# Windowed attention of a fused transformer kernel: from four windows of 32 queries against 64 keys to two halves of 64 queries against 96 keys

## The reference

```python
for i in range(6):
    x = attn_layer(shift_tokens(x), Wqkv[i], q_scale[i], k_scale[i], Wo[i]) + x
    x = ffn_layer(shift_tokens(x), ln_g[i], ln_b[i], W1[i], b1[i], W2[i], b2[i]) + x

def local_attention(q, k, v):            # w = 32, nw = n // 32
    bk2, bv2 = (look(bk), look(bv))      # each window of 32 keys behind the window before it
    ...
    mask = (it < jb) | (it > jb + w) | (jb == -1)
    sim = jnp.einsum('bhwie,bhwje->bhwij', bq, bk2) * QK_SCALE
    attn = jax.nn.softmax(jnp.where(mask, -max, sim), -1)
    return jnp.einsum('bhwij,bhwje->bhwie', attn, bv2)
```

## Time and the profile before

| | us |
|---|---|
| median of 3 runs | 3318.39 |
| lowest and highest | 3317.79, 3320.12 |
| the profiled execution, its own time | 3320.12 |
| its span, from the first to the last instruction | 3318.0 |
| mean granted clock of PE | 0.911 of full speed |
| steady state, four visits of the last stage | 67.68 |
| the last stage, about | from 1634 to 3315 |

### The profile page before, as it was taken

One profiled execution on the slowest core, in us unless ns is written; L12 is line 12 of the kernel. 1 busy time (PEld: TensorE's weight loads), 2 busy tenths in 40 slices (PEclk: granted clock), 3 DMA queues, 4 the chain that ended last, 5 costly groups with the idle time before them and its releaser, 6 DMA issues.

```text
span 3318.0 us, 85682 instructions
## 1 busy us (share of the span) xinstructions
PE 2877.0 (87%) x35131; PEld 1723.7 (52%) x35188; DVE 2383.9 (72%) x4250; ACT 1882.8 (57%) x5278; POOL 1208.9 (36%) x851
## 2 busy tenths in 40 slices
PE   4669857475979799999689999999999999999997
PEld 3444546452334423333256666666666666666664
DVE  4950279627960487777588888888888888888885
ACT  4222231126422246666468777787778777787775
POOL 0010000100000011111157766766776676676662
PEclk7569855587989989999889999999999999999999
DMA  2000000000000110000222233222332332322222
GB/s 101 2 1 0 36 2 3 1 1 0 0 0 0 34 44 25 24 22 22 92 63 66 65 76 93 62 72 64 97 77 65 97 77 66 95 61 62 60 65 51
DMA packets 48229, 153.18 MB, mean 46 GB/s; under 512 B 11552, under 2 KB 13856, under 8 KB 45952
## 3 DMA queue, kind: packets, MB, share of 16 engines
q1 hardware_dynamic: 47872, 148.11, 17.0%
HBM read 43.53 MB, written 5.44 MB: 15 GB/s over the span
## 4 chain that ended last, share of the span: by engine, by line
PE 65%; DVE 26%; ACT 2%; DVEq 2%; issue 2%; DMA 1%; POOLq 1%; ACTq 1%; SPq 0%; POOL 0%
PE ps L1481 10%; PE ps L648 7%; PE ps L1532 6%; PE ps L1499 5%; PE ps L1540 5%; DVE arena L1942 4%; DVE arena L972 4%; PE ps L1076 4%; PE ps L1104 4%; PE ps L1553 4%; PE ps L1091 3%; PE ps L1514 2%; PE ps L1559 2%; DVE arena L2022 2%; DVE pack_l L1935 2%
## 5 line engine op out<-in xcount | busy, mean ns | idle before, releaser
L1481 PE MATMUL ps<-arena 128*128 128x512 f32 x1152 | 560.2, 609 | 17.5 <-ACTq L1761 16.2
L2099 POOL TENSOR_TENSOR arena<-arena 128x1024 f32<-128x1024 f32 x190 | 448.3, 2360 | 145.5 <-DVE arena L1911 143.5
L1826 ACT ACTIVATE arena<-ps,arena 128x64 f32<-128x64 f32 x1536 | 457.0, 324 | 47.2 <-DVE arena L2022 44.1
L2105 POOL TENSOR_TENSOR arena<-arena 128x2048 f32<-128x2048 f32 x95 | 344.3, 3624 | 224.9 <-ACT arena L1768 219.8
L1241 DVE TENSOR_REDUCE arena<-ps 128x1 f32<-128x512 f32 x512 | 329.3, 685 | 77.2 <-PE ps L1076 72.1
L1203 ACT ACTIVATE arena<-ps 128x1024 f32<-128x1024 f32 x256 | 262.2, 1024 | 178.5 <-PE ps L1091 169.8
L1826 ACT ACTIVATION_READ_ACCUMULATOR arena<-ps,arena 128x1 f32 x1536 | 333.5, 217 | 0.0
L1906 DVE TENSOR_TENSOR arena<-ps,arena 128x1024 f32<-128x1024 f32 x192 | 235.0, 1224 | 110.1 <-PE ps L1481 95.6
L1481 PEld LDWEIGHTS ps<-arena 128*128 128x128 f32 x1152 | 197.0, 191 | 172.5 <-issue 158.0
L191 POOL TENSOR_SCALAR rstd<-mv 128x4 f32<-128x4 f32 x32 | 8.2, 255 | 718.4 <-DVE mv L178 718.4
L1532 PEld LDWEIGHTS ps<-arena 128*64 128x64 f32 x6144 | 189.6, 138 | 111.3 <-issue 111.3
(11 more groups left out here) (286 smaller groups left out, 5490.1 us busy)
## 6 DMA issues: line engine op xcount, KB each, us to landing
arena<-pack_l SPq DMA_DIRECT2D x144, 256.0 KB
arena<-grow SPq DMA_DIRECT2D x144, 256.0 KB
arena<-in_deep SPq DMA_DIRECT2D x6, 2649.5 KB, 10.7
arena<-pack_l SPq DMA_DIRECT2D x96, 128.0 KB
arena<-grow SPq DMA_DIRECT2D x84, 128.0 KB
arena<-in_rotary SPq DMA_DIRECT2D x6, 1024.0 KB, 7.5
pack_tern<-in_tern SPq DMA_DIRECT2D x2, 2888.0 KB, 10.7
arena<-scr_q SPq DMA_DIRECT2D x96, 48.0 KB
```

The source lines that it names most:

```text
L1481: last = T.matmul(m.ps[0:rows.stop - rows.start, at + half, :], f.xs[t % 2][:, rows], w.wqkv[:, j * INNER + half * BLK:j * INNER + (half + ...
L1826: last = A(f.prob[:, p, :], m.ps[:, 4 + j % 2, i * SPAN:(i + 1) * SPAN], ACT.Exp, bias=f.nmax[t % 2][:, p:p + 1], accum_out=f.rsum[t % 2][ ...
L2099: G.tensor_tensor(f.rot[t % 2][:, here], f.rot[t % 2][:, here], f.sin[:, here], ALU.add)
L2105: G.tensor_tensor(r, r, spread(f.ss[t % 2], DH), ALU.mult).then_inc(s["rotated"], 1)
```

## The change

The queries are taken in two halves of 64 instead of four windows of 32. A half sees 96 keys: its own 64 and the 32 before them, and the mask removes what lies outside the band. The scores of a bank hold 4 x 96 columns in place of 4 x 64. A head's probabilities are now one matrix of 128x96, which needs a transpose of its own, and comes out with keys on partitions 0 to 95, just as `heads` wants them: no spreading, one copy of 96x1024 for eight heads. The eight transposes of a `probs` call fill banks 0 and 1 together, and so PE waits before `probs(1)` until ACT has copied what `probs(0)` left there. Values need 96 rows a half, with two or three DMAs a visit. The heads' order inside the probabilities is that of the banks.

```diff
-    "const": [("ident", P), ("band", 64), ("band0", 64), ("cT", 2 * LAYERS)],
+    "const": [("ident", P), ("band", 96), ("band0", 96), ("cT", 2 * LAYERS)],
...
-SPAN = 2 * WIN
+SPAN = WIN + HALF
+ORDER = [h for half in range(2) for odd in range(2) for h in range(8 * half + odd, 8 * half + 8, 2)]
...
-    return sum(4 + (u % BT != 0) for u in range(t % 2, t + 1, 2))
+    return sum(2 + (u % BT != 0) for u in range(t % 2, t + 1, 2))
...
         for i in range(GROUP):
-            for w in range(WINS):
+            for half in range(2):
                 for e in range(2):
-                    k = 2 * j + i
-                    rows, queries = slice(DH * e, DH * e + DH), slice(WIN * w, WIN * (w + 1))
-                    last = T.matmul(m.ps[queries, 4 + e, i * SPAN:(i + 1) * SPAN], f.qT[rows, k, queries],
-                                    f.kT[t % 2][rows, k, WIN * w:WIN * w + SPAN], start=False, stop=True,
+                    h = ORDER[GROUP * (j + e) + i]
+                    rows = slice(DH * e, DH * e + DH)
+                    last = T.matmul(m.ps[HALF * half:HALF * (half + 1), 4 + e, i * SPAN:(i + 1) * SPAN],
+                                    f.qT[rows, h // 2, HALF * half:HALF * (half + 1)],
+                                    f.kT[t % 2][rows, h // 2, HALF * half:HALF * half + SPAN], start=False, stop=True,
                                     skip_group_check=True)
...
     def probs(j):
-
-        for i in range(GROUP):
-            last = T.transpose(m.ps[:, PROB_AT + j, i * P:(i + 1) * P], f.flat_prob[:, 4 * j + i, :], m.ident)
+        for i in range(8):
+            last = T.transpose(m.ps[0:SPAN, PROB_AT + i // 4, (i % 4) * P:(i % 4 + 1) * P], f.prob[:, 8 * j + i, :],
+                               m.ident)
...
-                                    f.v[t % 2][:, half, h * DH:(h + 1) * DH],
-                                    f.pT[:, h, HALF * half:HALF * (half + 1)], start=True, stop=True)
+                                    f.v[t % 2][0:SPAN, half, h * DH:(h + 1) * DH],
+                                    f.pT[0:SPAN, ORDER.index(h), HALF * half:HALF * (half + 1)], start=True, stop=True)
...
         if behind:
+            pe.wait_ge(s["p_copied"], 2 * t - 1)
             pe.wait_ge(s["normed"], 2 * t)
             probs(1)
...
-        for e in range(2):
-            for u in range(2):
-                to, got = f.turned_probs(0, e, u)
-                last = A(to, got, ACT.Copy)
-        last.then_inc(s["p_copied"], 1)
+        A(f.pT[0:SPAN, 0:8, :], wide(PROB_AT, SPAN).rearrange("p a (i b) -> p (a i) b", b=P),
+          ACT.Copy).then_inc(s["p_copied"], 1)
...
-    for u in range(2):
-        V.memset(f.pT_windows[SPAN * u:SPAN * (u + 1), :, :, 1 - u, :], 0.0)
...
-        for e in range(2):
-            for u in range(2):
-                to, got = f.turned_probs(1, e, u)
-                last = V.tensor_copy(to, got)
-        last.then_inc(s["p_copied"], 1)
+        V.tensor_copy(f.pT[0:SPAN, 8:16, :],
+                      m.ps[0:SPAN, PROB_AT:PROB_AT + 2, :].rearrange("p a (i b) -> p (a i) b", b=P))\
+            .then_inc(s["p_copied"], 1)
...
-        sp.dma_start(v[t % 2][WIN:SPAN, 0, :], raw[0:WIN, :]).then_inc(s["v_spread"][t % 2], 16)
-        sp.dma_start(v[t % 2][SPAN:P, 0, :], raw[0:SPAN, :]).then_inc(s["v_spread"][t % 2], 16)
-        sp.dma_start(v[t % 2][0:SPAN, 1, :], raw[WIN:WIN + SPAN, :]).then_inc(s["v_spread"][t % 2], 16)
-        sp.dma_start(v[t % 2][SPAN:P, 1, :], raw[HALF:P, :]).then_inc(s["v_spread"][t % 2], 16)
+        sp.dma_start(v[t % 2][WIN:SPAN, 0, :], raw[0:HALF, :]).then_inc(s["v_spread"][t % 2], 16)
+        sp.dma_start(v[t % 2][0:SPAN, 1, :], raw[WIN:P, :]).then_inc(s["v_spread"][t % 2], 16)
```

More of the change, by code:

```diff
@@ L1439 @@
 WIN = 32
-WINS = P // WIN
 HALF = P // 2
-SPAN = 2 * WIN
+SPAN = WIN + HALF
 KEYS = WIN + P
 FRONT = WIN + 1
+ORDER = [h for half in range(2) for odd in range(2) for h in range(8 * half + odd, 8 * half + 8, 2)]
 GROUP = 4
@@ L1509, in scores @@
         for i in range(GROUP):
-            for w in range(WINS):
+            for half in range(2):
                 for e in range(2):
-                    k = 2 * j + i
-                    rows, queries = slice(DH * e, DH * e + DH), slice(WIN * w, WIN * (w + 1))
-                    last = T.matmul(m.ps[queries, 4 + e, i * SPAN:(i + 1) * SPAN], f.qT[rows, k, queries],
-                                    f.kT[t % 2][rows, k, WIN * w:WIN * w + SPAN], start=False, stop=True,
+                    h = ORDER[GROUP * (j + e) + i]
[3 more added lines that the diff above has]
+                                    f.kT[t % 2][rows, h // 2, HALF * half:HALF * half + SPAN], start=False, stop=True,
                                     skip_group_check=True)
-                    if i == GROUP - 1 and w == WINS - 1:
+                    if i == GROUP - 1 and half == 1:
                         last.then_inc(s["scored"], 1)
     def probs(j):
-        for i in range(GROUP):
-            last = T.transpose(m.ps[:, PROB_AT + j, i * P:(i + 1) * P], f.flat_prob[:, 4 * j + i, :], m.ident)
+        for i in range(8):
+            last = T.transpose(m.ps[0:SPAN, PROB_AT + i // 4, (i % 4) * P:(i % 4 + 1) * P], f.prob[:, 8 * j + i, :],
+                               m.ident)
         last.then_inc(s["p_made"], 1)
@@ L1824, in exponentials @@
             for i in range(GROUP):
-                p = 8 * (j // 2) + 2 * i + j % 2
+                p = GROUP * j + i
                 last = A(f.prob[:, p, :], m.ps[:, 4 + j % 2, i * SPAN:(i + 1) * SPAN], ACT.Exp,
@@ L2021, in maxima @@
             dve.wait_ge(s["scored"], 4 * t + j + 1)
-            V.tensor_reduce(f.nmax[t % 2][:, 8 * (j // 2):8 * (j // 2) + 8].rearrange("p (i e) -> p e i", e=2)[:, j % 2, :],
+            V.tensor_reduce(f.nmax[t % 2][:, GROUP * j:GROUP * (j + 1)],
                             m.ps[:, 4 + j % 2, 0:GROUP * SPAN].rearrange("p (h k) -> p h k", h=GROUP), AX, ALU.max,
@@ L2237, in deep_setup @@
     f.pT = a.take(LH * P).rearrange("p (a b) -> p a b", b=P)
[L2238 to L2248, removed]
+    f.prob = a.take(LH * SPAN).rearrange("p (a b) -> p a b", b=SPAN)
     f.kT = [a.take(QB * KEYS).rearrange("p (a b) -> p a b", b=KEYS) for _ in range(2)]
@@ L2481, in band_masks @@
 def band_masks():
-    i, j = np.arange(P)[:, None], np.arange(2 * WIN)[None, :] - WIN
-    seen = (j <= i % WIN) & (j >= i % WIN - WIN)
-    first = seen & ((j >= 0) | (i >= WIN))
+    i, j = np.arange(P)[:, None], np.arange(96)[None, :] - 32
+    seen = (j <= i % 64) & (j >= i % 64 - 32)
+    first = seen & ((j >= 0) | (i >= 64))
     big = np.float32(-1e30)
```

## The result

The changed kernel takes 3380.4 us (median of four runs, 3378.4 to 3385.4) where the kernel before takes 3318.4 us (median of four as well): 1.019 times as long, with a 95% interval of 1.0175 to 1.020. The forecast was 3375 us.

A forecast was written before the change was run, and what follows sets the result against it. TensorE's own work list plus one 0.40 us wait per visit bounds the kernel. Stretch A +0.05 and stretch B +0.55 make +0.60 us a visit, +57 us over 95 visits: 3375 us, range 3342 to 3425 us.

The forecast's parts named there:

- Transposes: Sixteen probability transposes a visit in place of eight: +0.44 us in stretch A and +0.44 us in stretch B.
- Bands: Four bf16 band matmuls a visit grow from 256 to 384 columns: +0.11 us in each stretch.
- Scores: Score products, half as many and wider: 0.79 us a call as before, so 0, between -0.14 and +0.64 us.
- Rivals 1 and 2: Score calls at the heads' rate, 1.01 us (3417 us, chance 0.15); row halves not overlapping, 1.43 us (3497 us, chance 0.06).
- rival 3: Score calls cost by the instruction, 0.39 us a call: -8 us, 3311 us; chance 0.06.
- lower end of 3346 us: Low end of the forecast's own span: 0.65 us a score call, stretch A -0.12 us, stretch B +0.41 us.
- Heads: Head products contract 96 rows in place of 128, with the same moving columns: 0, between -0.1 and 0.
- The DVE path: VectorE's work through stretch A: copies -0.50 us, two maxima +0.27 us, from 3.87 to 3.64 us.
- Stretch A: Part of a visit from first band matmul to first head product, 3.87 us: +0.05 us, between 0 and +0.10.
- Stretch B: Rest of the visit, where TensorE never waits: bands +0.11, scores 0, transposes +0.44, together +0.55 us.
- The new wait: TensorE waits before the second transposes for ScalarE's copy of the first: 0.7 us of cover, cost 0.
- Work beside PE: ScalarE about 0 net, GpSimd +1.05 us and VectorE +0.27 us in free time, DMAs and memsets 0.

The follow-up runs named there:

- experiment 3: Changed kernel with every second probability transpose left out (output isn't the reference's): 3308.1 us, 0.9975 of the kernel before.
- experiment 4: Kernel before with each probability transpose issued twice to the same place: 3421.0 us, 1.031.
- 10: Changed kernel with each of its sixteen probability transposes a visit issued twice to the same place: 3546.0 us, 1.0688 of the kernel before.
- experiment 1: Changed kernel with the old score products, 32 of 32 queries against 64 keys per call on eight tiles: 3386.5 us, 1.0206 of the kernel before.
- experiment 2: Changed kernel with the second group of transposes in PSUM banks of its own, without the wait for ScalarE's copy: 3379.8 us, 1.0188 of the kernel before.
- experiment 5: Kernel before with two bf16 matmuls of 512 columns ahead of each group of four probability transposes: 3420.7 us, 1.0308.
- 7: Kernel before with the four copies of the second probabilities shared, two on VectorE and two on ScalarE: 3296.3 us, 0.993.
- 8: Kernel before with the copies shared between VectorE and ScalarE, and VectorE's two ahead of its second maxima: 3292.1 us, 0.9924.
- experiment 6: Kernel before with VectorE copying the second probabilities before its second maximum: 3315.3 us, 0.9994.

## Why the prediction was right, by its steps

- **Transposes** (+0.44 us in A, +0.44 in B): measured +0.42 to 0.44 and +0.44, +78 us over the stage. Experiments 3, 4 and 10 move the time by this term alone, down and up. This is the cause of the slowdown; the other terms together are -16 us.
- **Bands** (+0.11 and +0.11): +0.11 and +0.11, 20 us.
- **Scores** (0, between -0.14 and +0.64): +0.03 a call, 5 us. The nearest row was L1104's, four tiles. Rivals 1 and 2 would have shown 1.01 and 1.43 us, rival 3 0.39 us; the row is 0.82. Experiment 1 ran both shapes in the same surroundings, 0.79 and 0.82 us. There was some luck in 0.79 as a forecast: its rule, the stream and 0.14 us on top, would give 0.43 + 0.14 = 0.57 us for the old shape, which takes 0.79. So the rule held for four tiles and not for eight, and what sets a call's time is not shown. The prediction's lower end of 3346 us also has a slip: by its own sum A would be -0.09 and not -0.12 us, hence 3349 us.
- **Heads** (0): 2.02 us from start to start before and after, 191.7 us over the stage in both.
- **The DVE path** (3.87 to 3.64 us): 3.66 us in the median visit, measured where it binds, in experiment 3. Maxima grew by 0.135 us each (predicted 0.135), the copy takes 1.22 us as predicted.
- **Stretch A** (+0.05, between 0 and 0.10): +0.10, the upper end. I took the middle between two readings of PE's idle time (0.45 and 0.55 us); the scores' 0.03 and that choice make up the difference. This and the scores in B are the 5 us between 3375 and 3380.
- **Stretch B** (+0.55): 2.68/4 - 0.10 = +0.57.
- **The new wait** (0.7 us of cover, cost 0): cost 0, as experiment 2 shows, but with 1.66 us of cover (0.7 predicted). The step was wrong in one sign. I let ACT's copy start 0.44 us later because the transposes end later. ACT isn't waiting for them, it is busy until 2413.25 with two copies of 1.02 us of the turned keys and queries (L1778, L1780), and those follow `turn_rotated`, which comes before the added transposes; so relative to the bands the copy starts 0.44 us earlier. It changed nothing only because both answers are above zero.
- **Work beside PE** (0): the groups by line of ACT, DVE and PE's transposes (busy us, mean ns, idle before):

```profile
L1828 ACT ACTIVATE arena<-ps,arena 128x96 f32<-128x96 f32 x1536 | 497.9, 350 | 81.4 <-DVE arena L2017 81.3
L1523 PE MATMUL ps<-pack_const,arena 128*96 128x128 f32 x1536 | 203.0, 275 | 0.0
L2017 DVE TENSOR_REDUCE arena<-ps 128x4 f32<-128x384 f32 x384 | 195.3, 550 | 2.1 <-PE ps L1514 2.0
```

  POOL's normalisation takes 1.47 us (predicted 1.57), and PE waits for none of these between 1700 and 3300 us but once, 0.4 us. The transposes have no idle time in front of them in 1536 instructions.

What the forecast did not foresee didn't reach the changed kernel: the stalls at dense score calls. With the old score shape, the changed kernel would have had some of them and taken 3386.5 us (experiment 1), and the kernel before with as many transposes takes 3421 us (experiment 4), at the edge of my range. That the sum came out so close owes something to their absence, which no term of it covered.

## What to carry to other kernels

Where PE is busy without a gap, price each kind of its work by the start-to-start time of the nearest row, and not by the number of instructions or bytes: an edit that halves the score matmuls but doubles the fp32 transposes of 128 columns pays 0.11 us for each of them, while the score calls followed neither their instructions (halved) nor their stream (0.43 to 0.65 us) and went from 0.79 to 0.82 us. A wait that goes with it gives back only what it was worth (0.4 us a visit here). When a removed wait gains less than its length, sum PE's start-to-start times by kind of work over the whole stage; the missing part shows up as another line that grew. Before a new wait is costed, find out what its engine is doing until then, since a delay of its input may be no delay for it.

## What the hardware showed that I had not expected

- **Stalls without a releaser.** With the old score call (64 matmul and 64 weight-load instructions in 0.79 us) and a longer visit, PE stops for 1.1 to 2.2 us in 10 to 12 of 96 visits (experiments 4 and 5), and for 0.5 to 0.9 us in 9 in experiment 1. In the DMA records each of these 31 stalls between 1700 and 3300 us ends 2.3 to 2.8 us after a 16 KB packet of the instruction queue started, and that packet takes 0.9 to 1.3 us while the core's other transfers run. The DMA view of 2112 to 2120 us in experiment 4, which holds the stall shown there (queue: packets, MB, share of 16 engines):

```profile
q1 hardware_dynamic: 336, 1.05, 57.4%
q8 instruction: 1, 0.02, 1.0%
```

  That PE ran out of instructions there is what this suggests, and no run tried it by itself. The Trainium skill (Runtime: NRT & Kernel Launch, Instruction fetch mechanics) calls the crossing of a 16 KiB block mostly hidden; if the stalls are such crossings, it is hidden in the kernel before and after, which have none, and not in experiment 4 with its stalls of 2 us.
- **What decides when they come** stays open. It is not the number of instructions added (experiment 5), not the lack of idle time on PE (7 and 8 have hardly any, and no stalls), not the length of the visit alone (10). The new score call, half as many instructions in the same time, never had one: 0.82 us in every visit but the first of the kernel after and of experiments 2, 3 and 10. The DMA traffic differs too, and no run tried it by itself: the DMA engines' share from 1700 to 3200 us is 0.28 in experiment 4 with its long stalls, 0.21 in experiment 1 with its short ones, 0.21 in the kernel after and 0.30 in the kernel before, with none. So the traffic alone doesn't bring the stalls, but it may set how long they are.
- **The second score call at 0.94 us** in nearly all visits of experiment 6, and 0.79 us in 8, which has the same order on DVE, is open as well.
- **A call costs 0.8 us in either shape**: 12.3 ns an instruction on eight tiles of 64x32 with 64 columns, 25.6 ns on four tiles of 64x64 with 96.
